# Splitting the attention output into its fp16 halves on GpSimd before it is transposed

## The reference

```python
x = x + ln(softmax(q @ k.T + bias, null column, masks) @ v @ Wout, g_out)      # layer 0
#   q = l2norm(xn @ Wq), k = l2norm(xn @ Wk); bias[h, i, j] from a small MLP of i - j
x = x + ln(softmax((xn @ Wq) * scale @ k.T + fside[h, i, j]) @ v @ Wo, g_out)  # layer 1
x = x + moe(x, cond)                                                            # layers 2 and 3
```

## Time and profile before

| what | value |
|---|---|
| median of three runs | 1648.43 us (1646.07 to 1648.87) |
| the profiled execution's own time | 1648.25 us |
| its span, first to last instruction | 1646.4 us |
| busy: PE, DVE, ACT, POOL | 1441.4, 1406.3, 1150.6, 838.8 us |
| attention, first to last `o_n` | 66.9 to 1310.4 us |
| mean granted TensorE clock | 0.973 |

### The profile page before, as it was taken

How to read it: one execution, slowest core, us unless ns; L and a number is a source line. 1 busy time by engine, 2 the same in 40 slices (tenths; PEclk the granted TensorE clock), 3 DMA queues, 4 the chain that set the end, 5 groups by cost and what they waited for, 6 DMA issues and landing times.

```text
span 1646.4 us, 44788 instructions
## 1 busy us (share of the span) xinstructions
PE 1441.4 (88%) x15551; PEld 1064.3 (65%) x15551; DVE 1406.3 (85%) x3562; ACT 1150.6 (70%) x2957; POOL 838.8 (51%) x1654
## 2 busy tenths in 40 slices
PE   3567778888999999986788899999999989999998
PEld 2445556666777777765666677777777756666665
DVE  5467787899999999987788899999999979888887
ACT  3466667887888888877788888888999723333332
POOL 4768687664554545457775443433232266632222
PEclk8589899999999999999999999999999999999999
DMA  4011121220222213111221212222214001000000
GB/s 147 19 31 55 40 65 53 84 67 33 79 79 91 91 58 125 59 40 33 72 78 53 85 66 72 79 85 91 98 65 144 2 4 43 1 1 1 14 14 26
DMA packets 50754, 96.46 MB, mean 59 GB/s; under 512 B 3732, under 2 KB 27364, under 8 KB 50532
## 3 DMA queue, kind: packets, MB, share of 16 engines
q1 hardware_dynamic: 47988, 92.65, 17.2%
q10 hardware_dynamic: 2544, 0.94, 0.3%
HBM read 91.41 MB, written 2.17 MB: 57 GB/s over the span
## 4 chain that ended last, share of the span: by engine, by line
PE 54%; DVE 21%; issue 7%; ACT 6%; POOL 5%; DVEq 0%; ACTq 0%; POOLq 0%
PE tp L1728 8%; DVE biased L1210 7%; PE sc L1606 5%; DVE p_lo L1309 5%; PE sc L1407 4%; PE sc L1409 4%; PE sc L1408 4%; PE sc L1607 4%; DVE q_a L1242 3%; PE aux L1407 3%; PE op L1407 2%; PE aux L1409 2%; PE aux L1408 2%; PE tp L1407 2%; PE tp L1409 2%
## 5 line engine op out<-in xcount | busy, mean ns | idle before, releaser
L1309 DVE TENSOR_TENSOR p_lo<-tp,p_hi 128x384 f16<-128x384 f32 (+3 forms) x768 | 413.1, 553 | 90.1 <-ACT p_hi L902 80.7
L805 ACT ACTIVATE probs<-biased,neg_max 128x256 f32<-128x256 f32 (+7 forms) x512 | 395.2, 772 | 25.9 <-DVE neg_max L1210 23.7
L1728 PE MATMUL tp<-ident,probs 128*128 128x128 f32 x2304 | 389.7, 278 | 2.4 <-DVE p_lo L1309 1.8
L902 ACT ACTIVATE p_hi<-tp 128x384 f16<-128x384 f32 (+3 forms) x768 | 369.4, 491 | 28.1 <-PE tp L1728 14.3
L1606 PE MATMUL sc<-k_a,q_a 128*128 128x512 f16 (+3 forms) x768 | 254.6, 332 | 90.3 <-DVE neg_max L1210 70.6
L1407 PE MATMUL op<-v_s,p_hi 128*128 128x64 f16 x2304 | 285.2, 194 | 42.7 <-DVE p_lo L1309 27.4
L1728 PEld LDWEIGHTS tp<-ident,probs 128*128 128x128 f32 x2304 | 266.8, 142 | 29.0 <-issue 10.7
L1409 PE MATMUL op<-v_s,p_lo 128*128 128x64 f16 x2304 | 284.2, 194 | 0.0
L1408 PE MATMUL op<-v_s,p_hi 128*128 128x64 f16 x2304 | 284.2, 194 | 0.0
L1407 PEld LDWEIGHTS op<-v_s,p_hi 128*128 128x128 f16 x2304 | 215.6, 98 | 71.7 <-DVE p_lo L1309 48.6
L1607 PE MATMUL sc<-k_b,q_b 128*128 128x512 f16 (+3 forms) x768 | 242.5, 329 | 0.0
(11 more groups left out here) (311 smaller groups left out, 3508.6 us busy)
## 6 DMA issues: line engine op xcount, KB each, us to landing
bias<-rel_table SPq DMA_DIRECT2D x4, 2048.0 KB, 8.0
bias<-in_fside_16xSxS SPq DMA_DIRECT2D x4, 2048.0 KB, 8.6
bias<-rel_table SPq DMA_DIRECT2D x4, 1792.0 KB, 7.8
bias<-in_fside_16xSxS SPq DMA_DIRECT2D x4, 1792.0 KB, 7.1
bias<-rel_table SPq DMA_DIRECT2D x4, 1536.0 KB, 7.6
bias<-in_fside_16xSxS SPq DMA_DIRECT2D x4, 1536.0 KB, 6.7
bias<-rel_table SPq DMA_DIRECT2D x4, 1280.0 KB, 5.8
bias<-in_fside_16xSxS SPq DMA_DIRECT2D x4, 1280.0 KB, 6.5
```

Of the source, the lines that this page charges most:

```text
L805: ac.activation(probs[:, i % 2, 0:w], biased[:, i % 2, 0:w], ACT.Exp, bias=neg_max[:, u % 2, i % HU:i % HU + 1], scale=-1.0, accum_out=row ...
L902: ac.activation(p_hi[:, gi % 4, 0:nb * P], tp[gi % 2][:, 0:nb * P], ACT.Copy)\
L1309: ve.tensor_tensor(p_lo[:, gi % 4, 0:nb * P], tp[gi % 2][:, 0:nb * P], p_hi[:, gi % 4, 0:nb * P], ALU.subtract).then_inc(s["p_lo"], 1)
L1728: last = te.transpose(tp[gi % 2][:, jj * P:(jj + 1) * P], probs[:, n % 2, (j0 + jj) * P:(j0 + jj + 1) * P], ident[:, :])
```

## The change

The output is split into its halves in SBUF, before the transposes. POOL, after `o_n`, casts it to fp16 (`o_16[:, 0]`) and subtracts the cast from `o_n` for the low half (`o_16[:, 1]`), each of the three instructions waiting for the one before. PE transposes the four fp16 blocks, with an fp16 identity (`ident16`, cast once at the start), into the same PSUM bytes, read as fp16. ACT evicts all 512 fp16 columns in one instruction into `ot`. DVE's `ot_lo` is gone; the y product waits for ACT's `ot_in`. The wait of POOL for the former transposes (`s["ot"]`) moves from ahead of `o_n` to ahead of the cast.

```diff
@@ POOL, k == 1
                     pool.wait_ge(s["r_den"], u + 1)
+                    link(gp.tensor_tensor(o_n[:, :, :], o_raw[:, :, :],
+                                          r_den[:, :].unsqueeze(2).to_broadcast([P, HU, DH]), ALU.mult))
                     if u >= 1:
                         pool.wait_ge(s["ot"], u)
-                    gp.tensor_tensor(o_n[:, :, :], o_raw[:, :, :],
-                                     r_den[:, :].unsqueeze(2).to_broadcast([P, HU, DH]), ALU.mult)\
-                        .then_inc(s["o_n"], 1)
+                    o_f = o_n[:, :, :].rearrange("p h d -> p (h d)")
+                    link(gp.tensor_copy(o_16[:, 0, :], o_f))
+                    gp.tensor_tensor(o_16[:, 1, :], o_f, o_16[:, 0, :], ALU.subtract).then_inc(s["o_n"], 1)
@@ ACT, k == 2
-                        o_t = second[:, 0:UW].rearrange("p (c q) -> p c q", q=P)
-                        ac.activation(ot_hi[:, :].rearrange("p (c q) -> p c q", q=P), turned(o_t) if u < U0 else o_t,
-                                      ACT.Copy).then_inc(s["ot_hi"], 1)
+                        o_t = second.bitcast(F16)[:, 0:2 * UW].rearrange("p (c q) -> p c q", q=P)
+                        ac.activation(ot[:, :, :, :].rearrange("p c h q -> p (c h) q"), turned(o_t) if u < U0 else o_t,
+                                      ACT.Copy).then_inc(s["ot_in"], 1)
@@ DVE, k == 2
-                        dve.wait_ge(s["ot_hi"], u + 1)
-                        o_t = second[:, 0:UW].rearrange("p (c q) -> p c q", q=P)
-                        ve.tensor_tensor(ot_lo[:, :].rearrange("p (c q) -> p c q", q=P), turned(o_t) if u < U0 else o_t,
-                                         ot_hi[:, :].rearrange("p (c q) -> p c q", q=P), ALU.subtract)\
-                            .then_inc(s["ot_lo"], 1)
@@ PE, k == 2
-                        take(True, (s["ot_lo"], u + 1))
+                        take(True, (s["ot_in"], u + 1))
                         pe.wait_ge(s["o_n"], u + 1)
-                        o_f = o_n[:, :, :].rearrange("p h d -> p (h d)")
+                        if u == 0:
+                            pe.wait_ge(setup["ident16"], 1)
+                        o_t = second.bitcast(F16)
                         for cc in range(UW // P):
-                            last = te.transpose(second[:, cc * P:(cc + 1) * P], o_f[:, cc * P:(cc + 1) * P], ident[:, :])
+                            for hl in range(2):
+                                at_ = (cc * 2 + hl) * P
+                                last = te.transpose(o_t[:, at_:at_ + P], o_16[:, hl, cc * P:(cc + 1) * P], ident16[:, :])
```

More of the change, by code:

```diff
@@ L151, in model @@
         o_n = sb("o_n", [P, HU, DH])
-        ot_hi = sb("ot_hi", [P, UW], F16)
-        ot_lo = sb("ot_lo", [P, UW], F16)
+        o_16 = sb("o_16", [P, 2, UW], F16)
+        ot = sb("ot", [P, UW // P, 2, P], F16)
+        ident16 = sb("ident16", [P, P], F16)
         y_acc = sb("y_acc", [P, B, D])
@@ L266, in sems @@
             return {name: sem(part + "_" + name) for name in names.split()}
-        setup = sems("setup", """mhalf ident rel place ones penalty big nss nrinv
+        setup = sems("setup", """mhalf ident ident16 rel place ones penalty big nss nrinv
                     mt cb lg lgh half vec var root u tanh h pt t mm mid stats rstd n tanh2 h2
@@ L276, in model @@
                     x_st x_rs xn xt xt_hi xt_lo xr_hi xr_lo kv kv_act kv_r kv_d kv_v k_dup kt k_hi k_lo
-                    d_null p_null denom r_den o_null o_raw o_n ot ot_hi ot_lo y y_s y_acc
+                    d_null p_null denom r_den o_null o_raw o_n ot ot_in y y_s y_acc
                     y_st y_rs y_n x_new""")
@@ L489, in _ @@
                              pattern=[[-1, P]], channel_multiplier=1).then_inc(setup["ident"], 1)
+            pool.wait_ge(setup["ident"], 1)
+            gp.tensor_copy(ident16[:, :], ident[:, :]).then_inc(setup["ident16"], 1)
             link(gp.iota(rel_i[:, :], [[-P, TILES]], base=S - 1, channel_multiplier=-1))
@@ L1287, in small @@
                                                         ALU.mult, ALU.subtract).then_inc(s["null_t"], 1)
-                    if k == 2 and 0 <= m - 1 < NU:
-                        u = m - 1
-                        dve.wait_ge(s["ot_hi"], u + 1)
-                        o_t = second[:, 0:UW].rearrange("p (c q) -> p c q", q=P)
-                        ve.tensor_tensor(ot_lo[:, :].rearrange("p (c q) -> p c q", q=P), turned(o_t) if u < U0 else o_t,
-                                         ot_hi[:, :].rearrange("p (c q) -> p c q", q=P), ALU.subtract)\
-                            .then_inc(s["ot_lo"], 1)
                     r, step_, at_ = in_round(n)
@@ L1613, in _ @@
                     take(False, (s["y_s"], u + 1))
-                    pe.wait_ge(s["ot_lo"], u + 1)
+                    pe.wait_ge(s["ot_in"], u + 1)
                     if u % U0 == 0:
@@ L1618, in _ @@
                         rows_ = hg * (UW // P) + cc
-                        last = three(first[:, 0:D], ot_hi[:, cc * P:(cc + 1) * P], ot_lo[:, cc * P:(cc + 1) * P],
+                        last = three(first[:, 0:D], ot[:, cc, 0, :], ot[:, cc, 1, :],
                                      wo[layer][:, 0, rows_, :], wo[layer][:, 1, rows_, :],
```

## The result

The changed kernel took 1662.88 us (median of four runs, 1661.30 to 1665.95) against 1648.25 us before: 1.0093 times as long, 95% interval 1.0076 to 1.0111. The forecast was 1660 us. The profiled execution has a span of 1661.0 us (1646.4 before).

A forecast was written before the change was run, and what follows sets the result against it. Narrow stages were taken as set by waits between engines, often POOL's queue, wide ones by PE and DVE together. 1648.25 less 9 gained plus 20 lost gave 1659.3, said as 1660 us; range 1642 to 1675.

The forecast's parts named there:

- The sum: Whole run: 1648.25 less 9 gained plus 20 lost gives 1659.3, said as 1660 us.
- The gain of 9 us: DVE's removed ot_lo, mostly in wide tiles: 6.9 + 0.7 + 3 kept, less 1.6 for ACT's longer eviction.
- the discount to 80%: Between 297 and 740 us, only 6.9 of ot_lo's 8.6 us on the chain were counted as gained.
- The prices: Per instruction: cast 405 ns, difference 672, eviction 598; POOL's queue 1.12 us longer per unit; PE's four transposes nothing extra.
- 1.25 us of lateness: At PE's transposes where they wait for POOL: start 2.02 us after o_n's start instead of 0.76.
- The loss of 20 us: Narrow units, from PE's lateness and POOL's longer queue: 14.5 in layer 0, 10.7 in layer 1, 25.2 reduced to 20.
- a fifth: Estimated deduction from the narrow-unit loss for earlier row maxima and other inputs being ready: 25.2 becomes 20 us.
- The shares of the two ways: Per narrow unit, the larger of delay through PE's late transposes and q_r's delay in POOL's queue, if on the chain.
- Rival 1: Late output is absorbed, only places where POOL is the chain cost, and the change wins: 1640 to 1646 us; 15%.
- Rival 2: Units 1 to 26 and 64 to 88 each pay the full 1.12 us: up to 1696, half 1668; 20%.
- Rival 3: Half the lateness is swallowed and 12 us gained, so both cancel: 1646 to 1651 us; 12%.
- Rival 4: PE stands more in narrow stages and its 1.2 GHz share grows: 2 to 5 us on top; 3%.

The follow-up runs named there:

- load_late: Kernel before the change, plus cast and difference on POOL behind o_n, read by nobody, product signalled to PE only after them; 1678.79 us, 1.0183.
- high_only: Changed kernel, but POOL writes the product straight into fp16 and the low half is constant zero, left out of the output; 1637.79 us, 0.9943.
- wide_only: Changed kernel's split only in tiles 4 to 7 of each layer, tiles 0 to 3 done as before the change; 1636.64 us, 0.9937.
- evict_last: wide_only with ACT's output eviction in tiles 4 to 7 moved behind the second p_hi; 1647.88 us, 1.0000.
- load_early: Kernel before the change, plus the unread cast and difference on POOL behind o_n, with the product signalling PE at once; 1669.38 us, 1.0139.
- load_behind: load_early with the unread cast and difference moved behind q_n, ahead of d_null and the query copy; 1683.96 us, 1.0220.

## Why the prediction was right, point by point

The mechanism was right: the pair lengthens POOL's queue and delays PE in narrow tiles, and the removed difference pays in wide ones. That the total came within 3 us of the forecast is in part luck, because both of its terms were too small and their errors pulled in opposite directions.

- **The sum.** Forecast 1659.3, said as 1660; measured 1662.88, 14.6 us above before where 11 were worked out. Between the two traces the loss is 27.8 us where 20 were said, and the giving back 12.5 where 9 were said. The experiments add up less well: load_late's loss of 31.6 less high_only's gain of 9.4 would be 22, by medians. With load_late's shortest run (23.8 above before) it is 14.4, so that the agreement rests on one run of four.
- **The gain of 9 us.** high_only has 9.4, wide_only 10.6. The way it was divided, 6.9 in layer 0's wide tiles and 3 in layer 1's, compares with 9.9 and 2.6 to 2.9 between the two traces. The 8.6 us of layer 0 that I called a ceiling were reached or passed (9.0 in wide_only, 10.4 in high_only, unit 28 to 63), so the discount to 80% had no ground. What made up for it is layer 1's narrow tiles, where high_only loses 2.5 us and 0.7 were to be gained. The step "in layer 1 about half gain nothing because p_hi comes 0.06 too late" was seen at unit 113. That ACT alone holds the rest back was too simple: evict_last shows PE behind it.
- **The prices.** The durations were all within 10 ns. The lengthening of POOL's queue was not: 1.21 us per unit instead of 1.12, because the next instruction starts 0.77 us after the difference (190.37 to 191.14), where I had taken 0.64. PE's four transposes cost what two did. Of the 1.25 us of lateness, o_n's start to the end of the difference is 1.83 and the gap behind it 0.15, together 1.98 against 0.76: 1.22.
- **The loss of 20 us.** This is the term that was too small. Before I took a fifth off, it was 14.5 in layer 0 and 10.7 in layer 1; the traces have 14.8 and 13.0. The fifth was an estimate without a row, and no such giving back is seen in narrow tiles. The price has a share: with 1.21 in place of 1.12 the 14.5 become 15.7, by estimate. The growth from unit 63 to 88, forecast as 8 to 10 us, was 13.0. In layer 1 the longer eviction may have a share that I had left out of this term, up to 2.5 us by high_only.
- **The shares of the two ways.** I took in each unit the larger of PE's lateness and POOL's queue. Before load_early I put the queue at 10 us in layer 0 and 2 in layer 1; it shows the queue alone at +14.9 in layer 0 and 5.6 in layer 1's narrow tiles, with the product's signal not late. So POOL's queue can carry all of layer 0 and some two fifths of layer 1's 13.0 us. No run has the lateness without the queue, so whether "the larger of the two" is the right rule stays open.
- **Rival 1, absorbed,** fell: unit 24 was 11.7 us late. **Rival 2, POOL the bound of every narrow unit,** is right on the mechanism and wrong on the size: 27.8 of its 57 us came, so about half is absorbed. load_behind, with the pair where no pause follows, comes nearer to it (36 us). **Rival 3** fell. **Rival 4, the clock:** the granted clock from 70 to 300 us was 0.93 before and, from 70 to 312, 0.90 after; PE's busy share fell from 73% to 70%, and the lower mean says that 1.2 GHz was granted for a larger share. The first row is of before, the second of the changed kernel, the third of load_behind (70 to 325 us); columns as in the earlier trace rows:

```profile
70.00:300.00 230.00, 167.93 (x1667) 123.89 (x1666) 171.01 (x546) 158.39 (x522) 171.49 (x370) 0.93 0.16 49
```

```profile
70.00:312.00 242.00, 170.21 (x1711) 129.43 (x1710) 163.50 (x521) 160.66 (x519) 198.60 (x418) 0.90 0.15 47
```

```profile
70.00:325.00 255.00, 179.71 (x1662) 130.96 (x1660) 170.98 (x544) 157.65 (x520) 197.59 (x419) 0.87 0.15 44
```

The sum of busy times is not the loss here: POOL has 27 us more in a stretch that is 12 longer. How much of the 12 is the clock's was not isolated; PE was busy for 2.3 us more there, with 44 more products, and for 11.8 us more in load_behind with about as many products as before.

## What to carry to other kernels

An engine at 51% of the span can be the bound of a stage: read its own order of time there, look for pauses, and ask which instruction behind the new one others wait for. An edit that moves work from a full engine to a half-full one should be priced stage by stage, and where it pays in one stage and costs in another, made only where it pays: here that turned a loss of 14.6 us into a gain of 10.6. Do not take a discount for "it will be absorbed" without a pause in the trace to absorb it. And an instruction that is removed frees two things, its engine's time and the buffer that it read; ask of both who was waiting.

## What I had not expected of the hardware

A DVE subtraction over 256 columns took 281 ns with both sources in fp16 (one in PSUM, one in SBUF) and 413 with the PSUM source in fp32, both written in fp16. And load_behind moved two POOL instructions of 1.1 us together from right behind o_n to behind q_n, in the same queue, and took 14.6 us more than load_early.
